# End of attention in a fused MoE, attention, MoE kernel: VectorE's routing chain moved six steps earlier, its sixteen second rows given to GpSimd, ScalarE's rows and two groups of TensorE products shifted

## The reference

```python
x = x + 0.5 * ffn(layernorm(x))       # 8 experts, top 2, hidden width 352
x = x + attention(layernorm(x))       # 16 heads of width 8, softmax over 256 keys, no causal mask
x = x + 0.5 * ffn(layernorm(x))       # the same expert weights again

# ffn: the router picks two experts per token
scores = softmax(xf @ gate_w.T)
_, sel = top_k(scores + expert_bias, 2)
top_scores = take_along_axis(scores, sel)
# each (token, choice) pair is sorted by expert, scaled by its score, and run through
h = silu(xe @ w1[e]) * (xe @ w3[e])
out = h @ w2[e]                       # and added back at its token
```

## Time and profile before

| | |
|---|---|
| median of 3 runs | 737.61 us (736.56 to 738.97) |
| the profiled execution | 737.8 us, span 736.0 us |
| TensorE busy | 621.3 us (84%) |
| VectorE busy | 446.4 us (61%) |
| ScalarE busy | 390.6 us (53%) |
| GpSimd busy | 303.1 us (41%) |
| mean granted TensorE clock | 0.953 |

### The profile page before, as it was taken

How to read it: one execution, slowest core, us unless ns; L and a number is a source line. 1 busy time by engine, 2 the same in 40 slices (tenths; PEclk the granted TensorE clock), 3 DMA queues, 4 the chain that set the end, 5 groups by cost and what they waited for, 6 DMA issues and landing times.

```text
span 736.0 us, 14989 instructions
## 1 busy us (share of the span) xinstructions
PE 621.3 (84%) x5080; PEld 475.7 (65%) x5080; DVE 446.4 (61%) x1164; ACT 390.6 (53%) x912; POOL 303.1 (41%) x312
## 2 busy tenths in 40 slices
PE   6399999999979778899899998899999999999100
PEld 6388999988857434455554554456989899999100
DVE  6955733235456989899999999973676322233211
ACT  1625764444422577778777787783457544444000
POOL 6067714565433373044000010005566077776474
PEclk9999999999999899999999999989999999999655
DMA  8358978787982454435334443016678878887322
GB/s 263 100 165 222 252 225 237 224 239 207 286 231 81 153 147 148 125 117 166 110 116 139 125 130 103 3 58 198 179 211 249 228 218 245 246 250 208 100 78 64
DMA packets 116586, 126.02 MB, mean 171 GB/s; under 512 B 12512, under 2 KB 99168, under 8 KB 116384
## 3 DMA queue, kind: packets, MB, share of 16 engines
q1 hardware_dynamic: 98544, 101.20, 45.7%
q0 software_dynamic: 9088, 18.63, 10.2%
q10 hardware_dynamic: 8880, 5.25, 2.3%
HBM read 89.37 MB, written 35.39 MB: 170 GB/s over the span
## 4 chain that ended last, share of the span: by engine, by line
PE 53%; DVE 24%; issue 6%; DMA 6%; POOL 5%; ACT 4%; SPq 1%; POOLq 0%; ACTq 0%; DVEq 0%
PE banks L684 13%; DVE mx L816 10%; PE banks L656 9%; PE banks L672 8%; PE banks L665 8%; POOL rows L588 4%; PE banks L1128 4%; PE banks L646 2%; PE banks L471 2%; ACT PT L1143 2%; DMA WR<-in_experts 2%; PE banks L1012 2%; PE banks L1101 1%; DVE resid L803 1%; DVE split L809 1%
## 5 line engine op out<-in xcount | busy, mean ns | idle before, releaser
L568 POOL DMA_INDIRECT xe<-routed_rows,idx x156 | 151.6, 972 | 224.7 <-PE banks L646 85.7
L816 DVE TENSOR_REDUCE mx<-banks 128x2 f32<-128x512 f32 x256 | 163.4, 683 | 8.9 <-PE banks L1103 7.7
L1143 ACT ACTIVATE PT<-banks 128x512 f32<-128x512 f32 x256 | 140.5, 604 | 36.4 <-PE banks L1114 34.1
L588 POOL DMA_INDIRECT rows<-slots_out,slot x128 | 124.0, 969 | 72.2 <-issue 27.8
L737 DVE TENSOR_TENSOR hidT<-banks,act 96x256 f32<-96x256 f32 (+1 forms) x92 | 34.9, 380 | 188.2 <-ACT act L718 187.9
L684 PE MATMUL banks<-WR,hidT 128*128 128x128 f32 x936 | 119.8, 275 | 0.6 <-ACT ye L727 0.6
L684 PEld LDWEIGHTS banks<-WR,hidT 128*128 128x128 f32 x936 | 111.9, 191 | 2.9 <-issue 1.0
L656 PE MATMUL banks<-xeT,WR 128*128 128x256 f32 (+1 forms) x368 | 86.1, 356 | 8.0 <-issue 3.8
L672 PE MATMUL banks<-xeT,WR 128*128 128x256 f32 (+1 forms) x368 | 82.8, 347 | 0.0
L665 PE MATMUL banks<-xeT,WR 128*96 128x256 f32 (+1 forms) x368 | 82.5, 347 | 0.0
L1128 PE MATMUL banks<-PT,V 128*32 128x256 f32 x1024 | 73.4, 407 | 4.5 <-ACT oT L1190 3.8
(11 more groups left out here) (160 smaller groups left out, 894.9 us busy)
## 6 DMA issues: line engine op xcount, KB each, us to landing
WR<-in_experts SPq DMA_DIRECT2D x92, 544.0 KB
stacks<-split SPq DMA_DIRECT2D x32, 384.0 KB
slots_out<-ye SPq DMA_DIRECT2D x156, 64.0 KB
QS<-stacks SPq DMA_DIRECT2D x64, 112.0 KB
KS<-stacks SPq DMA_DIRECT2D x64, 112.0 KB
routed_rows<-xn ACTq DMA_DIRECT2D x16, 256.0 KB, 5.3
routed_rows<-xn SPq DMA_DIRECT2D x12, 256.0 KB, 2.3
xe<-routed_rows,idx POOLq DMA_INDIRECT x156, 4.4
```

Source lines behind the costliest of these rows:

```text
L568: eng.indirect_dma_start(xe[:, i % XR, a, :], None, routed_rows[h], bass.IndirectOffsetOnAxis(ap=idx[h][:, tile:tile + 1], axis=0))\
L588: eng.indirect_dma_start(rows[:, k, t, :], None, slots_out[h], bass.IndirectOffsetOnAxis(ap=slot[h][:, k, t:t + 1], axis=0))\
L816: eng.tensor_reduce(mx[:, :, e, pair], maxima_bank(f)[:, :].rearrange("p (q n) -> p q n", q=2), AX.X, ALU.max).then_inc(s_max, 1)
L1143: eng.activation(PT[:, u % 4, 1 - k].rearrange("p t n -> p (t n)"), PS[f % 3], ACT.Exp, scale=scale).then_inc(s_exp2, 1)
```

## The change

VectorE's ticks 11 and 23 to 34 are handed out in steps 98 to 110 instead of 104 to 116: the coefficients come at step 109 instead of 115. Ticks 47 to 62 follow at steps 116 to 122 instead of 118 to 125; tick 80, the indices, stays at step 126. The 16 rows of choice 1 are made by GpSimd, between its last power (`root_gpsimd`) and its gathers, as soon as the coefficients are there. ScalarE's exponential goes from step 105 to 99, and its 16 rows from two each in steps 117 to 124 to one each in steps 111 to 118 and two each in steps 119 to 122. TensorE's counts go from step 117 to 115, its inverse products from step 125 to 124. SP stores the rows in another order, those of choice 1 mostly first.

```diff
-        def rows_vector(eng):
+        def rows_gpsimd(eng):
 
             eng.wait_ge(s_coef, 2 * 3)
             eng.wait_ge(s_comb, GC * HALVES)
...
-            for k, c in ((0, 0), (0, 1), (0, 2), (1, 0), (0, 3), (1, 1), (1, 2), (1, 3)):
+            for k, c in ((1, 0), (0, 0), (1, 1), (1, 2), (0, 1), (1, 3), (0, 2), (0, 3)):
...
             root_gpsimd(pool, 8, 0)
+            for _ in rows_gpsimd(pool):
+                pass
...
-            attention_scalar(act, side, spans((105, 105, 17), (117, 117, 23), (118, 124, 2), (125, 125, 1)))
+            attention_scalar(act, side, spans((99, 99, 17), (110, 110, 21), (111, 118, 1), (119, 122, 2), (123, 123, 1)))
...
-            attention_tensor(pe, side, spans((117, 117, 39), (125, 125, 35)))
+            attention_tensor(pe, side, spans((115, 115, 39), (124, 124, 35)))
...
-            side, made = chained(route_norm(dve, 8, 0, 1), route_vector(dve, 2, 0)), rows_vector(dve)
+            side = chained(route_norm(dve, 8, 0, 1), route_vector(dve, 2, 0))
...
-                             (made, spans((124, 124, 1), (125, 125, 2), (126, 126, 1)), None),
-                             (side, spans((72, 73, 1), (80, 81, 1), (88, 89, 1), (96, 96, 3), (97, 97, 1), (104, 104, 12),
-                                     (106, 107, 1), (109, 109, 1), (111, 113, 1), (114, 114, 2), (115, 115, 3),
-                                     (116, 116, 13), (118, 119, 2), (120, 121, 3), (122, 123, 2), (125, 125, 2)), PAIRS * (BATCH - 1) + 6))
+                             (side, spans((72, 73, 1), (80, 81, 1), (88, 89, 1), (96, 96, 3), (97, 97, 1),
+                                          (98, 98, 12), (100, 107, 1), (108, 108, 2), (109, 109, 1), (110, 110, 13),
+                                          (116, 117, 2), (118, 119, 3), (120, 122, 2)), PAIRS * (BATCH - 1) + 6))
```

## The result

The changed kernel is slower: 742.97 us against 737.09 us (medians of six runs each), ratio 1.0086, 95% interval 1.005 to 1.0122. Two more measurements of the same code gave 1.0090 (1.0052 to 1.0128) and 1.0093 (1.0059 to 1.0128). The forecast was 739.3 us with a range up to 742.0.

A forecast was written before the change was run, and what follows sets the result against it. VectorE was taken to bound the kernel up to step 114, then ScalarE, slow-clocked TensorE and two nearly equal closing chains. Terms +2.4 - 0.63 + 0 - 0.14 = +1.6 us gave 739.3 us; own range 738.0 to 740.8, with rivals 736.2 to 742.0.

The forecast's parts named there:

- forecast 2.4: VectorE's last negation, near step 114: 2.4 us later, from 3.66 us of earlier work less 1.25 us absorbed in waits.
- the first distance: Between VectorE's negations at steps 98 and 106: to grow from 12.8 to over 15.5 us if the forecast is right.
- GpSimd's rows: Sixteen second rows moved from VectorE to GpSimd: 0.5 us each, 8 us together, hidden up to 2.2 us a row.
- the data's chain: Stage end: VectorE's last second rows, their store and GpSimd's two gathers; ahead of TensorE's own order by 0.14 us, the gain.
- the inverse products: TensorE's 32 products moved from step 125 to 124: 4.87 us either way, sum 0, bounds -0.4 and +0.5 us.
- The sign of the sum: Whole kernel: slower by 1.6 us, with a chance of 0.49 of staying within 0.3% of 737.6 us.
- The absorbed part of the 3.66 us: VectorE's coefficient work moved ahead of the last maxima: 1.25 of its 3.66 us to disappear into VectorE's waits.
- the three waits: VectorE's waits in the last two batches of maxima, 0.28, 0.51 and 0.46 us, taken as room for 1.25 us of work.
- The -0.63 us behind step 114: Gain from fewer ScalarE rows in steps 117 to 121 and VectorE free sooner for TensorE; bounds -0.3 and -1.3 us.
- rival C: TensorE's clock falls earlier, in the two batches VectorE bounds: 1.6 us more, 740.9 us; chance 0.15.
- C's own sign: The granted clock dipping once between 444 and 475 us would decide for the earlier clock fall.
- Rival B: TensorE keeps 2.4 GHz at 486 to 492 us and after the inverse products: some 4.2 us gained, 735.1 us; chance 0.10.

The follow-up runs named there:

- e5: The changed kernel measured a second time, no code change; ratio 1.0090 to the kernel before.
- e3: The changed kernel with the inverse products back at step 125; ratio 1.0054 to the kernel before, mean 740.29 us.
- e8: The changed kernel with one small bf16 product of 128 columns added in each of steps 98 to 114; ratio 1.0107 to the kernel before.
- e11: The changed kernel with the counts back at step 117 and VectorE's ticks from 47 on at their old steps; ratio 1.0074, mean 742.21 us.
- e15: The changed kernel measured a third time, no code change; ratio 1.0093 to the kernel before.
- e1: The kernel before with only VectorE's ticks 11 and 23 to 34 early, and ScalarE's exponential at step 99; ratio 1.0062, mean 740.56 us.
- e14: The changed kernel with two keep-pace products instead of one (none in 115 to 117) in each of steps 115 to 123; ratio 1.0068, mean 740.95 us.
- e4: The changed kernel with two more unread 128x128 products in each of steps 98 to 114; ratio 1.0186 to the kernel before.
- e12: The kernel before with second rows by GpSimd and the inverse products at step 124; ratio 1.0006, mean 736.45 us.
- e13: The kernel before with only second rows by GpSimd and the new order of stores, measured again; ratio 1.0004, mean 736.04 us.
- e2: The kernel before with only second rows by GpSimd and the new order of stores; ratio 1.0018.
- e6: The kernel before with second rows by GpSimd, ScalarE's exponential at step 99, and ticks 11, 23 and 24 at steps 98, 101 and 103; ratio 1.0011.

## Why the prediction was wrong

**What held.** VectorE's work sets the distances between the negations; the last one comes later by 2.75 us (2.93 and -0.18), forecast 2.4, and the first distance "over 15.5" was 15.73. GpSimd's rows are hidden: 7.0 us for sixteen, 0.44 us a row, forecast 0.5. The gathers start behind the indices, the data's chain was worth nothing, the inverse products cost nothing with the ticks at their old places, and taking the counts back changed nothing (742.21 against 742.43 us, standard error 0.7). The sign of the sum was right, which the forecast hid by calling the case no change.

**The terms that were mis-sized.** The absorbed part of the 3.66 us was 0.9, not 1.25. Of the three waits the changed kernel's VectorE has lost two; the one of 0.28 us, for TensorE's turning in the first batch, is still there (at 443.86 us). That is 0.35 us.

The -0.63 us behind step 114 came out as a loss. The prediction took VectorE's negation as the mark of the stage up to step 114, because TensorE stood waiting for it: the turning of the maxima started 0.51 us behind it, and the values ahead of that had started 2.10 us before it, without a wait:

```profile
470.17 1.07 PE L1128 MATMUL banks<-PT,V 128*32 128x256 f32 x16
```

With the ticks done by step 110, VectorE takes its last maxima back to back, while TensorE is still behind: in e5 it waits 0.67 us for ScalarE's read, starts these values only 0.48 us ahead of the negation, and turns the maxima 1.39 us behind it. The second turning of values at step 117 was to start as late as before and not to wait for VectorE; it starts 5.19 us behind the negation instead of 3.93, and waits 0.44 us. What follows was to start 0.4 to 0.5 us sooner. The fourth group of values starts 14.21 us behind the negation where it was 13.35 (485.62 us in the earlier trace rows). All of this is at full clock, and it repeats: 13.35 or 13.36 us in the eight profiles without the early ticks, 14.20 or 14.21 in e3, e5, e8, e11 and e15, and 14.30 in e1, where rows and counts are at their old steps. (In the changed kernel's first profile and in e14 a low stretch or added products lie in between, in e4 TensorE is the bound.) So by that point the changed kernel is 3.6 us later at full clock, 2.75 by the negation and 0.86 by TensorE behind it. The prediction had 2.4 - 0.63 = 1.8 us for the whole stage, most of the 0.63 ahead of this point. The moved rows and counts are worth 0.09 us there, e1 against the others, and not 0.63.

From there to the load the profiles do not agree, as the clock falls in this part: with the same low time behind step 114 the changed kernel takes 20.9 us in e5 against 22.4 before (10.2 us low), and 21.2 in e15 against 23.2 in e12 (13.6), but e3 and e11 take 20.5 and 21.0 against 20.2 in e13 (6.8). What the change is worth in this part is open. Over the whole stage at 10.2 us of low time, e1, e5 and e11 average 67.09 us, the kernel before, e2 and e6 63.84: 3.25 us.

**The step that failed with the largest share is the clock.** The prediction took the low time as given. It priced rival C, a dip in VectorE's two batches, at 1.6 us, which was right (16.95, 16.84 and 16.75 us against 15.42 where one fell into the second batch, 17.20 against 15.73 in the first), but gave it a chance of 0.15 as an alternative to the forecast. It is no alternative, it comes on top of the same later negation. By C's own sign, a dip before 475 us, the changed kernel's profile was its case (472.9 us), and its 740.9 us were too low even so. Of the eight profiles with VectorE's ticks early (e4 left out), five have a low stretch that begins within 33 us of the negation of step 98: the changed kernel, e1, e11, e14 and e15. Of the eight with the ticks at their old places or nearly so, none has; there the first begins 41 us behind it or later. Over its 23 executions the changed kernel spends 8.5 us more at 1.2 GHz than the kernel before (standard error 1.3). At 0.37 us each these are 3.1 us. With the 3.25 us of the stages at equal low time this makes 6.4 us; measured are 6.4, with a standard error of 0.7. The 0.37 is a slope between executions of one kernel; that it holds between kernels is assumed. That a thinner TensorE is what brings the clock down is argued from e4 and e14, which filled it and had less low time, and not shown: e8's light fill left 73.7 us.

**Rival B** was read as one event that comes or not. The same code has 6.8 us in one profile and 10.2 in another (e13, e2), with 1.8 us between their stages. Two sums of the prediction do not come out either: B's terms, three times 0.86 us and as much again, make 5.2 us and not 4.2; and the lower end of its own range, 738.0 us, does not follow from its bounds, which give 736.2 (0 for the first term, -1.3 for the second). Neither changes the outcome.

**What stays open.** The changed kernel lies 2.1 us (standard error 1.1) above e3_inverse, which differs from it in the step of the inverse products alone. Its low time is 6.2 us higher (standard error 2.2), and at 0.37 us each that is 2.3 us, the whole difference; the same holds for e1_ticks (6.1 us more low time, 1.9 us of time). With the ticks at their old places the same step of the products changed neither the time nor the low time (e12 against e2 and e13: -0.1 and -2.2 us, standard errors 0.9 and 2.2). So of the 8.5 us of low time some 2 come with the early ticks and some 6 seem to come with the products at step 124 beside them (e11, which has both, lies between, 72.6 us with a standard error of 1.6), at under three standard errors and with no experiment that shows why. A lead is in the profiles: the low stretch that the products are followed by lasts 7 us or more in eight of the nine profiles with them at step 124, and 4 us in six of the eight with them at step 125.

e14 gave back 7.4 us of low time, worth 2.7 us; less the 0.8 us that its twelve added products had cost by the fourth group of values, 1.9 would be expected, and 1.3 was measured (standard error 1.0). What makes the clock fall in one execution and not in the next was not found.

## What to carry to other kernels

Work that is moved to free an engine at the end of a stage is paid where it lands: count it in full against the engine that bounds that place, and take a wait as room only as far as a run shows that it goes. Where one engine's mark stands for the pace of all, look at whether the next engine waits at it, and ask whether it still will after the move: here TensorE had stood waiting for the negation, and afterwards came 0.9 us late to it. If the move thins TensorE's work, price the extra time at low clock as part of the forecast, not as a rival, and from the scatter of the executions (time against mean granted clock), not from one profile. And before an experiment moves one piece alone, ask what the other pieces had cleared out of its way: the inverse products at 124 cost nothing with the rows on GpSimd and 9.7 us without.

## What the runs showed of the hardware

GpSimd's product and sum over 128 columns of float32, with two scalars per partition, takes 0.44 us, against 0.34 us on VectorE. Beside them VectorE's maxima were unchanged, 678 to 693 ns (ten of them), against 682 to 693 in the same batch of the kernel before. Two routing operations with two SBUF inputs were slower, 0.57 and 0.36 us against 0.41 and 0.29:

```profile
465.34 0.57 DVE L351 TENSOR_TENSOR_SCAN upto<-CT,taken 128x128 f32<-128x128 f32 x1
465.95 0.36 DVE L353 TENSOR_TENSOR place<-upto,taken 128x128 f32<-128x128 f32 x1
```

That is the rule of the Trainium skill, "GPSIMD Engine Reference", section 1 (SBUF interfaces shared, contention where VectorE's instruction has two SBUF inputs): the trace agrees, at a price of 0.23 us for both. In e1_ticks the same two stand at the same steps with GpSimd idle, and take 0.41 and 0.29 us. Not each is held, though: in e2_gpsimd the running sum began 0.30 us behind GpSimd's first row and took 0.41 us, and only the subtraction behind it 0.36.

The granted clock takes either of its two levels at places that differ from execution to execution of the same code: in the three profiles of the changed kernel the first low stretch of the stage begins 18, 32 and 47 us behind the negation of step 98. One place is the same in all seventeen profiles: during the 32 inverse products (78 columns each, 4.8 to 4.9 us in a row, TensorE busy throughout) or within 0.7 us of their end the clock is at 0.50, whatever it was before them. Executions of one kernel spread over 13 us (730.9 to 743.8 us in the kernel before), and in most kernels the longer ones are those with more time at 1.2 GHz.
